# Softmax denominators by TensorE from every probability tile, instead of from pairs summed by GpSimd

## The reference

```python
scores = jnp.einsum('bhnd,bhmd->bhnm', q, k) * scale      # 12 x 1024 x 1024
attn = jax.nn.softmax(scores.astype(jnp.float32), axis=-1)
out = jnp.einsum('bhnm,bhmd->bhnd', attn, v)
```

## Time and profile before

| | |
|---|---|
| median of the three runs | 1538.79 us |
| the profiled execution | 1540.33 us |
| its span, first to last instruction | 1538.7 us |
| mean granted TensorE clock (1 is full) | 0.919 |
| busy: TensorE products | 1336.6 us (87%) |
| busy: ScalarE | 746.8 us (49%) |
| busy: VectorE | 704.8 us (46%) |
| busy: GpSimd | 426.4 us (28%) |

### The profile page before, as it was taken

One profiled execution on the slowest core, in us unless ns is written; L12 is line 12 of the kernel. 1 busy time (PEld: TensorE's weight loads), 2 busy tenths in 40 slices (PEclk: granted clock), 3 DMA queues, 4 the chain that ended last, 5 costly groups with the idle time before them and its releaser, 6 DMA issues.

```text
span 1538.7 us, 25061 instructions
## 1 busy us (share of the span) xinstructions
PE 1336.6 (87%) x9022; PEld 1038.9 (68%) x9023; DVE 704.8 (46%) x1287; ACT 746.8 (49%) x1362; POOL 426.4 (28%) x336
## 2 busy tenths in 40 slices
PE   5978989776999999993979999986999499999996
PEld 3534444454999999992544444443888299999996
DVE  3365567673242333334675556658323333233331
ACT  2736666612563556452553666554531245544642
POOL 4135555404111111115323555541000411111111
PEclk9969999975999999996977999997999599999998
DMA  7720000055263453614150000003003714235411
GB/s 275 198 52 2 1 1 2 1 204 183 33 217 78 143 153 97 196 24 125 36 123 1 1 2 1 1 2 125 1 1 116 264 26 144 53 121 153 143 31 26
DMA packets 63919, 129.21 MB, mean 84 GB/s; under 512 B 6144, under 2 KB 51279, under 8 KB 63855
## 3 DMA queue, kind: packets, MB, share of 16 engines
q1 hardware_dynamic: 50766, 95.20, 18.1%
q0 software_dynamic: 13088, 33.17, 9.6%
HBM read 89.23 MB, written 28.00 MB: 76 GB/s over the span
## 4 chain that ended last, share of the span: by engine, by line
PE 64%; DVE 11%; ACT 7%; issue 6%; DMA 6%; POOL 2%; DVEq 1%; POOLq 0%; SPq 0%; ACTq 0%
PE bank L1285 15%; PE bank L1296 11%; PE bank L1207 7%; PE bank L1169 6%; PE bank L1087 6%; PE bank L1147 4%; PE bank L1313 3%; PE bank L1330 3%; ACT probs L967 3%; DVE row_max L659 3%; DMA residual<-y_tile,tokens_out 3%; PE bank L1184 3%; DVE w_lo L806 2%; POOL grouped L446 2%; DMA out_x<-y_tile,tokens_out 2%
## 5 line engine op out<-in xcount | busy, mean ns | idle before, releaser
L1285 PE MATMUL bank<-xT_tile,w 128*128 128x128 f32 x2880 | 334.9, 278 | 3.9 <-DVE xT_tile L790 2.4
L1285 PEld LDWEIGHTS bank<-xT_tile,w 128*128 128x128 f32 x2880 | 332.8, 194 | 5.7 <-DVE xT_tile L790 3.2
L659 DVE TENSOR_REDUCE row_max<-bank 128x1 f32<-128x1024 f32 x192 | 228.9, 1220 | 156.9 <-PE bank L1147 120.3
L492 POOL TENSOR_TENSOR pairs<-probs 128x1024 f32<-128x1024 f32 x94 | 223.5, 2379 | 217.0 <-PE bank L1184 164.8
L967 ACT ACTIVATE probs<-bank 128x1024 f32<-128x1024 f32 x192 | 196.2, 1024 | 145.9 <-PE bank L1207 128.2
L1018 ACT ACTIVATE h_tile<-bank,b 128x128 f32<-128x128 f32 x480 | 168.7, 365 | 173.5 <-PE bank L1285 167.0
L1296 PE MATMUL bank<-w_hi,h_lo 128*128 128x384 f32 x480 | 165.9, 346 | 19.7 <-DVE h_lo L813 19.7
L1147 PE MATMUL bank<-k_stack,q_stack 96*128 96x512 f32 x384 | 140.3, 472 | 33.1 <-DVE row_max L659 19.8
L469 POOL DMA_DIRECT2D x_tile<-grouped x40 | 22.8, 571 | 518.2 <-DVE whose_next L818 491.6
L1296 PE MATMUL bank<-w_lo,h_hi 128*128 128x384 f32 x480 | 163.4, 340 | 0.0
L1207 PE MATMUL bank<-q_stack,k_stack 97*128 97x512 f32 x384 | 148.6, 465 | 17.0 <-ACT probs L967 16.7
(11 more groups left out here) (197 smaller groups left out, 1716.2 us busy)
## 6 DMA issues: line engine op xcount, KB each, us to landing
w<-in_l0w SPq DMA_DIRECT2D x16, 2304.0 KB, 14.0
w<-in_l1w SPq DMA_DIRECT2D x12, 2304.0 KB, 11.1
grouped<-rows POOLq DMA_DIRECT2D x2, 4825.0 KB, 24.7
x_tile<-grouped POOLq DMA_DIRECT2D x44, 193.0 KB, 2.7
q_stack<-stage SPq DMA_DIRECT2D x64, 96.0 KB, 2.2
k_stack<-stage SPq DMA_DIRECT2D x48, 96.0 KB, 2.2
w<-in_mlp_w SPq DMA_DIRECT2D x2, 2304.0 KB, 10.9
w_qkv<-in_l0qkv SPq DMA_DIRECT2D x1, 1728.0 KB, 9.9
```

The costliest lines, as they stand in the source:

```text
L492: pool.tensor_tensor(pairs[:, g % PAIR_RING, :], probs[:, 2 * g % P_RING, :], probs[:, (2 * g + 1) % P_RING, :], ALU.add).then_inc(named(" ...
L659: ins = dve.tensor_reduce(row_max[:, h, t:t + 1], bank[:, pair:pair + 2, :], AX.XY, ALU.max)
L1285: ins = pe.matmul(bank[:, f % 4, 0:P], w1[at][:, c, f * P:(f + 1) * P], xT_tile[:, c, :], start=(c == 0), stop=(c == NC_ - 1))
```

## The change

A tile's ones product is issued in `values`, for each of the 96 tiles, right behind its values product and from `probs` itself. `denominators`, `sum_pairs`, the `pairs` buffer and the semaphores `pair` and `den_mm` go. ScalarE no longer waits for them, neither before an exponential that overwrites a tile nor before the copies; it waits for `pv`, which is raised behind both products.

```diff
-        pairs = sb("pairs", [P, PAIR_RING, T], F32, att)
...
-    def sum_pairs(pool, n):
-        for g in range(PAIRS):
-            pool.wait_ge(*since(n, "exp", 2 * g + 2))
-            if g >= PAIR_RING:
-                pool.wait_ge(*since(n, "den_mm", g - PAIR_RING + 1))
-            pool.tensor_tensor(pairs[:, g % PAIR_RING, :], probs[:, 2 * g % P_RING, :],
-                               probs[:, (2 * g + 1) % P_RING, :], ALU.add).then_inc(named("pair"), 1)
...
-            sum_pairs(pool, n)
             pool.wait_ge(*since(n, "proj_add", NT))
...
                     act.wait_ge(*since(n, "pv", u - P_RING + 1))
-                    act.wait_ge(*since(n, "pair", min((u - P_RING) // 2 + 1, PAIRS)))
...
                     act.wait_ge(*since(n, "pv", NT * h))
-                    act.wait_ge(*since(n, "den_mm", NT // 2 * h))
...
             act.wait_ge(*since(n, "pv", NT * H))
-            act.wait_ge(*since(n, "den_mm", PAIRS))
...
                     ins = pe.matmul(bank[D * j:D * j + D, 6 + h % 2, 0:PART], v_tok[:, kt, D * head:D * head + D],
                                     probs[:, u % P_RING, PART * j:PART * j + PART],
                                     start=(kt == 0), stop=(kt == NT - 1), skip_group_check=True)
-                if u >= 2 * PAIRS:
-                    for j in range(HPC):
-                        ins = pe.matmul(bank[D * j:D * j + D, 6 + h % 2, PART:2 * PART], ones_v[:, :],
-                                        probs[:, u % P_RING, PART * j:PART * j + PART],
-                                        start=False, stop=(kt == NT - 1), skip_group_check=True)
-                ins.then_inc(named("pv"), 1)
-
-            def denominators(g):
-
-                h, i = divmod(g, NT // 2)
-                pe.wait_ge(*since(n, "pair", g + 1))
                 for j in range(HPC):
                     ins = pe.matmul(bank[D * j:D * j + D, 6 + h % 2, PART:2 * PART], ones_v[:, :],
-                                    pairs[:, g % PAIR_RING, PART * j:PART * j + PART],
-                                    start=False, stop=(i == NT // 2 - 1), skip_group_check=True)
-                ins.then_inc(named("den_mm"), 1)
+                                    probs[:, u % P_RING, PART * j:PART * j + PART],
+                                    start=False, stop=(kt == NT - 1), skip_group_check=True)
+                ins.then_inc(named("pv"), 1)
...
                     values(u - 2)
                     values(u - 1)
-                if u >= 4:
-                    denominators(u // 2 - 2)
             values(H * NT - 2)
-            denominators(PAIRS - 1)
             values(H * NT - 1)
```

More of the change, by code:

```diff
@@ L65 @@
 P_RING = 4
-PAIR_RING = 2
 PART = T // HPC
 EVACS = 2 * HPC
-PAIRS = H * NT // 2 - 1
 LEAD = 13
@@ L247, in program @@
             "mx_mm": H * (NT + 1), "mx_read": H * NT, "neg": H, "shift": H, "st": H * NT, "exp": H * NT,
-            "pv": H * NT, "pair": PAIRS, "den_mm": PAIRS, "acc_copy": EVACS * H,
+            "pv": H * NT, "acc_copy": EVACS * H,
             "att": NC_ * NT, "proj": NT, "proj_add": NT, "bo": NT}
```

## The result

The kernel after the change takes 1572.29 us (median of 4 runs, 1571.91 to 1572.42); four runs of the kernel before on the same chip gave 1538.72 (1538.02 to 1539.53). The ratio is 1.0218 with a 95% interval of 1.02 to 1.0235: 33.6 us slower. The forecast was 1574.9, range 1566 to 1583. The profiled execution took 1572.42 us, with a span of 1570.8 and a mean granted clock of 0.922.

The account below looks back on a forecast made before the run. TensorE's queue was taken to set the pace in both attention loops, with GpSimd waiting for it. Added ones products gave 17.7 and 18.4 us, together 36.1, on the 1538.79 median: 1574.9 us, range 1566 to 1583.

Parts of the forecast that it names:

- The price: In the loops, a ones product of 8 instructions takes 0.43 us on the chain, on a tile or a pair alike.
- The 40 turns: Turns u = 4 to 82 of each attention get one more ones product each: 40 x 0.43 = 17.2 us.
- All of it on the chain: In the 40 turns the odd exponential ends first and covers nothing: 0.43 us each, with bounds from 0.12 to 0.43.
- Rival (c): The odd exponential partly covers the product: 0.12 instead of 0.43 in 80 turns, 25 us less, 1550; chance 0.03.
- GpSimd's adds at nothing: Removing GpSimd's 94 adds, 223.5 us of work, takes 0 from the chain.
- rival (b): VectorE sets the pace somewhere, so 8.6 us of its products slowed beside adds come back: 27.5 slower, 1566.3; chance 0.05.
- The turn u = 2: First turn with values in each attention gets two ones products: 0.86 us if the clock rises at the same moment.
- The last turns: Turns u = 84 to 94 get one product each; replaying both queues gave +0.3 us per attention, bounds 0 to 2.2.
- The waits removed: Copies of a head no longer wait for its last ones product: 0.7 us back in the first loop, 0 in the second.
- Rival (a): Half clock makes it dearer: all 94 products on the chain and one more fall, 43.7 us, 1582.5; chance 0.08.
- What stands outside the loops: Stages outside the loops keep their lengths; one changing by over 3 us would show the forecast wrong.
- rival (d): Faster: later stages meet another TensorE clock, at 320 to 400 and 700 to 814, at most 53 us saved, 1522; chance 0.02.

Follow-up runs that it names:

- Experiment 4: Kernel after, with the values products of every odd tile left out (output not the attention's): 1507.67 us, ratio 0.9803; only its turns are read.
- Experiments 5 to 7: Ones products moved ahead of odd scores: kernel before, all turns, 1538.04 us; kernel before, two turns in four, 1531.88; kernel after, in those two turns, 1554.06.
- experiment 3: Kernel after, with GpSimd's adds put back, their sums unread, ScalarE waiting for them before overwriting a tile: 1572.07 us, ratio 1.0218 to the kernel before.
- experiment 8: Kernel before, with fifteen unused VectorE maxima behind each loop so that later stages begin about as late as after the change: 1574.39 us.
- experiment 9: Kernel before, with GpSimd also adding two pairs to one, 27 ones products for 49, placed in turns with room: 1526.85 us, ratio 0.9915.
- experiment 5: Kernel before, with the pair's ones product moved between the scores of the even and the odd tile: 1538.04 us, ratio 1.0011.

## Why the prediction was right, and where it was not

**The price, right.** A ones product takes 0.43 us on the chain whether its operand is a tile or a pair. The 40 turns took 16.86 and 17.16 us more, where 16.5 and 17.2 were forecast (17.2 less the 0.7 of the waits). Experiment 4 shows that it is a price per group of eight instructions.

**All of it on the chain, right.** The odd exponential covers none of it: the earlier trace rows had TensorE 0.31 us late already. Rival (c), 0.12 each, is ruled out by turns of 4.37 us. Experiments 5 to 7 refine this: in the forecast's place nothing is covered, in the gaps of two turns in four a part is.

**GpSimd's adds at nothing, right**, by experiment 3. The forecast's sign that line 675's products would all lie near 0.29 us came true (291 to 293 ns), and rival (b) with it falls: those 8.6 us were real and not on the chain.

**The turn u = 2, right on average, and in part by luck.** 0.86 in each attention was forecast; 0.50 and 1.42 were measured. Each kernel has a second trace: the means of the two differ by 0.62 in the first attention (4.45 and 4.85 before, 4.95 and 5.58 after) and by 0.97 in the second (5.07 and 5.61, 6.49 and 6.12). Together that is 1.6, where 1.72 was forecast, but a single trace moves by 0.4 to 0.6 with the moment of the clock's rise. That the rise comes at the same moment as before, as the forecast assumed, doesn't hold from one execution to the next.

**The last turns, too small.** Forecast +0.3, measured +0.67 and +0.87 (+0.72 and +0.89 between the second traces). Two of six turns grow by the whole 0.43 or 0.44, as the replay had it. The other four, where exponentials are waited for, together give back 0.2 in the first attention and nothing in the second; the replay had them give back 0.6. Why they give back less was not tested.

**The waits removed, nearly right.** Where the copies delayed a turn before, it grew by 0.34 instead of 0.43; together 0.3 us came back in the first loop, where 0.7 were forecast.

**Rival (a)**, a clock that makes it dearer, did not come. The fall at the end of the second loop is in the first trace of both kernels and in neither second one. With it the turns u = 80 and 82 together grow by 0.89 us (9.57 to 10.46), without it by 0.86 (7.99 to 8.85). The fall itself costs 1.6 us in either kernel, as the rival had priced it, but the change brought no further one. Nor did it take one away, as (a) also allowed: the kernel before has a trace without that fall too, and one in which it comes in the first attention instead.

**What stands outside the loops was costed at nothing, and that was wrong by a little, or by scatter.** The forecast named a change of over 3 us in a stage there as a sign against it. The second routing, from its first transposition to that of the first expert tile, was 3.5 us shorter in the first pair of traces (47.1 to 43.6) and 0.9 in the second (45.0 to 44.1). All stages outside together took 5.4 and 2.1 us less in the two pairs, and 2.0 to 3.3 between the means of several traces. The loops alone grew by 36.4 us between the means, 0.3 more than forecast, and the time by 33.6, 2.5 less than forecast. So what the total missed is of the size of this term.

Where the difference lies, TensorE's clock differs. The second routing, first 13 us, in the kernel before and its repeat:

```profile
1184.00:1197.00 13.00, 12.46 (x76) 12.09 (x74) 4.16 (x15) 5.31 (x10) 0.50 (x2) 0.67 0.85 309
```

```profile
1183.00:1196.00 13.00, 10.78 (x77) 10.42 (x75) 5.76 (x37) 5.30 (x10) 0.50 (x2) 0.74 0.84 308
```

and in the kernel after and its repeat:

```profile
1221.00:1234.00 13.00, 9.43 (x81) 9.01 (x79) 7.49 (x48) 5.52 (x11) 0.50 (x2) 0.89 0.84 304
```

```profile
1219.00:1232.00 13.00, 9.56 (x75) 9.20 (x73) 6.88 (x45) 5.51 (x11) 0.50 (x2) 0.77 0.86 312
```

Six products that choose the experts take 1.29 us at 1192.33 in the kernel before and 0.73 at 1226.51 in the kernel after. Over the ten traces whose routing sees the same data, this stage takes 46.8 to 47.1 us where the clock granted over the whole stage was 0.54, 44.1 to 45.0 where it was 0.56 to 0.58, and 43.6 to 43.8 where it was 0.61. The fourth tile of the second experts' stage lost to the clock too (experiment 8). Its first tile went the other way, from 16.4 and 16.7 us to 17.6. So it is the mechanism of rival (d), later stages that meet another clock, in another place than the rival named and at a few us instead of 53; in 320 to 400 and 700 to 814 the clock was 0.66 and 0.77 and stayed near that. What sets the moment of the fall in a given execution is open, and so is how much of the difference is the change's doing: experiment 9, whose program for TensorE is nearer to that of before, has the long routing and the short tile.

## What to carry to other kernels

Price an added TensorE product by the pieces of the chain, not by the mean of its records (0.43 us for a group of eight, where one record has 383 ns), and ask of each place in the queue how long the engine waits there: here 0.31 us late behind the values, about 0.15 us of room ahead of the odd scores, and more in every second turn. Work that an idle engine does to halve another's is worth keeping where that other one sets the pace, even if the idle engine then looks busy; doing more of it, with the products where there is room, won 12 us here, until GpSimd itself set the pace in the densest turns. A stage that the change leaves alone may still move by some us, so a trace of each kernel should be repeated, and the granted clock compared, before a stage is argued from.

## What the runs showed of the hardware that was not expected

The first group of eight after products of another shape costs more: 0.57 us on the chain, where those behind it take 0.43, in the turns of every kernel here (121.93 and 122.50 in the chain after; 205.67 in experiment 5, where the ones product had moved behind the maxima and paid this). The Trainium skill, TensorEngine Tiling (Array Packing), "Key Properties", says that a change of tiling mode drains TensorE; the runs fit that, with 0.14 us more on the chain, but they don't tell a drain from another cost of the change of shape.

TensorE's clock rises at the start of a loop at moments that differ between two executions of one kernel: the turn u = 2 took 4.95 and 5.58 us in the first attention and 6.49 and 6.12 in the second, with the same instructions. A fall at the end of a loop, worth 1.6 us, comes in one execution of a kernel and not in the next. Such moments are 1 to 2 us of the scatter of a trace.
